# Gated cross-attention in four layers: the block of value matmuls moved ahead of the pair's last row maximum in TensorE's order

## The reference

```
x = x + tanh(g_xattn[l]) * attention_l(layernorm(x), ctx_1024, ctx_1024)
x = x + tanh(g_ffn[l])   * ffn_l(layernorm(x))
```

```
scores = jnp.einsum('blhe,bshe->bhls', q, k)
A = jax.nn.softmax(scale * scores, axis=-1)
ctx = jnp.einsum('bhls,bshd->blhd', A, v).reshape(Bsz, Lq, H * E)
out = ctx @ Wo + bo
```

## Time and profile before

| | |
|---|---|
| time, three runs | 1059.38, 1055.20, 1058.17 us; median 1058.17 us |
| span of the profiled execution, first to last instruction | 1052.7 us (its device time is not given apart from this; the three runs lie 2.5 to 6.7 us above the span) |
| instructions in the trace | 17430 |
| PE busy | 971.8 us (92%), 6530 matmuls |
| PE weight loads | 574.6 us (55%) |
| DVE busy | 774.0 us (74%) |
| ACT busy | 488.9 us (46%) |
| POOL busy | 290.5 us (28%) |
| mean granted TensorE clock | 0.969 of 2.4 GHz |
| costliest groups | reductions L2343: 640 of 681 ns mean, 397.1 us; exponents L1208: 320 of 1022 ns, 312.3 us; maxima L1567: 640, of 477 and 494 ns mean; values L1601: 2560 in the trace, 381 ns mean |

### The profile page before, as it was taken

How to read it: one execution, slowest core, us unless ns; L and a number is a source line. 1 busy time by engine, 2 the same in 40 slices (tenths; PEclk the granted TensorE clock), 3 DMA queues, 4 the chain that set the end, 5 groups by cost and what they waited for, 6 DMA issues and landing times.

```text
span 1052.7 us, 17430 instructions
## 1 busy us (share of the span) xinstructions
PE 971.8 (92%) x6530; PEld 574.6 (55%) x6530; DVE 774.0 (74%) x1445; ACT 488.9 (46%) x708; POOL 290.5 (28%) x439
## 2 busy tenths in 40 slices
PE   8897987999999977999689999999999999899998
PEld 4333353444444454999254444445788788644446
DVE  4989888999999631454489899995664645699956
ACT  2672331477777721121027777776312212347763
POOL 3656710133343203002302433322500400013230
PEclk9998989999999977999899999999999999999999
DMA  6889912103320323995341233201254242110001
GB/s 205 271 266 311 361 35 69 43 25 115 124 86 23 98 85 115 327 374 186 90 150 47 63 84 83 62 9 42 87 192 141 84 140 100 28 45 13 8 2 40
DMA packets 79181, 121.81 MB, mean 116 GB/s; under 512 B 9733, under 2 KB 52904, under 8 KB 79090
## 3 DMA queue, kind: packets, MB, share of 16 engines
q1 hardware_dynamic: 59278, 79.29, 24.3%
q10 hardware_dynamic: 19044, 39.22, 10.7%
q0 software_dynamic: 768, 2.10, 0.6%
HBM read 92.10 MB, written 27.81 MB: 114 GB/s over the span
## 4 chain that ended last, share of the span: by engine, by line
PE 67%; DVE 20%; DMA 5%; issue 3%; ACT 2%; POOL 2%; SPq 0%; DVEq 0%; ACTq 0%; POOLq 0%
PE bank L1601 15%; PE bank L1567 15%; PE bank L1822 12%; DVE arena L2343 10%; PE st_bank L1752 4%; PE bank L1764 4%; DMA kparts<-arena 3%; PE st_bank L1586 3%; PE st_bank L1822 2%; PE bank L1361 2%; PE st_bank L1515 1%; PE bank L1655 1%; PE bank L1620 1%; DVE bnst L1925 1%; PE st_bank L1891 1%
## 5 line engine op out<-in xcount | busy, mean ns | idle before, releaser
L2343 DVE TENSOR_REDUCE arena<-bank 128x1 f32<-128x512 f32 x640 | 397.1, 681 | 33.7 <-PE bank L1567 32.8
L1208 ACT ACTIVATE arena<-st_bank 128x1024 f32<-128x1024 f32 x320 | 312.3, 1022 | 137.1 <-PE st_bank L1586 136.0
L1567 PE MATMUL bank<-g_a 64*128 64x512 f32 x480 | 181.5, 477 | 11.7 <-DVE arena L2343 3.3
L1601 PE MATMUL bank<-arena,vaug 128*9 128x256 f32 (+2 forms) x2560 | 168.5, 381 | 1.3 <-ACT arena L1208 1.3
L1567 PEld LDWEIGHTS bank<-g_a 64*128 64x128 f32 x480 | 73.2, 183 | 124.9 <-DVE arena L2343 100.3
L1822 PE MATMUL bank<-g_a,g_w 128*128 128x512 f32 x512 | 117.3, 390 | 1.1 <-POOL g_a L959 1.1
L1586 PE MATMUL st_bank<-g_a 64*128 64x512 f32 x480 | 115.3, 417 | 0.0
L1822 PEld LDWEIGHTS bank<-g_a,g_w 128*128 128x128 f32 x512 | 95.9, 188 | 21.9 <-POOL g_a L959 2.0
L926 POOL COPY arena<-arena 8x32 f32<-8x32 f32 x160 | 34.8, 217 | 259.4 <-issue 137.2
L1601 PEld LDWEIGHTS bank<-arena,vaug 128*9 128x9 f32 (+2 forms) x2560 | 55.8, 92 | 75.2 <-issue 39.7
L1567 PE MATMUL bank<-g_x,g_a 64*128 64x512 f32 x160 | 63.4, 494 | 9.6 <-DVE arena L2343 3.5
(11 more groups left out here) (329 smaller groups left out, 1442.3 us busy)
## 6 DMA issues: line engine op xcount, KB each, us to landing
arena<-in_glu_w SPq DMA_DIRECT2D x39, 512.0 KB, 3.2
arena<-kv_table SPq DMA_DIRECT2D x11, 1024.0 KB, 7.6
ctxT<-in_glu_w ACTq DMA_DIRECT2D x22, 512.0 KB, 5.9
arena<-in_w SPq DMA_DIRECT2D x20, 512.0 KB, 5.9
kparts<-arena ACTq DMA_DIRECT2D x12, 512.0 KB, 5.4
arena<-in_w ACTq DMA_DIRECT2D x12, 512.0 KB, 3.4
xnT<-kv_table SPq DMA_DIRECT2D x5, 1024.0 KB, 8.0
g_a<-kparts SPq DMA_DIRECT2D x24, 192.0 KB
```

The lines of the kernel that those rows point to most:

```text
L1208: act.activation(prob[sl % PROBS], st_bank[sl % 2][:], ACT.Exp, scale=scale).then_inc(exp_ready, 1)
L1567: pe.matmul(bank[TURN_BANKS[place % 3]], Qc[gi % KQ_BUFS][rows, qt * P:(qt + 1) * P], Kc[gi % KQ_BUFS][rows, half * CH:(half + 1) * CH], s ...
L1601: ins = pe.matmul(bank[7][at:at + dh + 1, 0:D], vaug[l][:, b * KT + 2 * m + i, h0 + hh, :], tiles[:, a], start=(m == 0 and i == 0), stop=( ...
L2343: dve.tensor_reduce(mxh[gi % 2][:, col, hf:hf + 1], bank[TURN_BANKS[place % 3]], AX.X, ALU.max).then_inc(max_red, 1)
```

## The change

In `schedule`, the call that adds the pair's last row maximum moves from in front of the values step to behind it. Nothing is added or removed, and the other engines' lists keep their order, since VectorE has no values step and ScalarE neither maxima nor values.

```diff
@@ -182,9 +182,9 @@
             steps.append(("score", g, kt))
-            maxima(LEAD + HG * sl)
             if sl % 2 and sl >= VALUES_LAG:
                 steps.append(("values", (sl - VALUES_LAG) // KT, (sl - VALUES_LAG) % KT // 2))
+            maxima(LEAD + HG * sl)
             if kt == COPY_SLOT and g:
                 steps.append(("copy", g - 1))
```

## The result

| | before | changed |
|---|---|---|
| median of six runs | 1057.04 us | 1083.68 us |
| lowest to highest | 1053.88 to 1059.38 | 1079.92 to 1088.68 |
| span of the profiled execution | 1052.7 us | 1078.2 us |
| mean granted clock | 0.969 | 0.974 |

The changed kernel is slower: ratio 1.0265, 95% interval 1.0238 to 1.0293. In medians it is 26.6 us, and the interval reaches from 25.2 to 31.0 us. The forecast was 1084, 25.9 us more.

A forecast was written before the change was run, and what follows sets the result against it. TensorE and VectorE waiting for each other bound the kernel at 2.68 us a pair; 119 lengths of 2.92 and 14 of 3.51 make 396.6 us against 370.7, adding 25.9 to 1058.2: 1084 us, range 1069 to 1091.

The forecast's parts named there:

- The closed chain: In the attentions, TensorE and VectorE wait for each other in turn; one loop sets a regular pair's 2.68 us.
- The wait removed: Before the values: the last maximum's 0.49 us and the 0.73 of first reduction and semaphore leave the path.
- The wait that takes its place: At the next pair's third maximum: waiting for the last reduction closes a new loop of 2.92 us, 0.24 more.
- Group's end: Pairs where VectorE finishes a group: its extra 0.38 us is hidden, so they go from 2.82 to 2.92.
- Context: Pairs with a context: four transposes add 0.59 us to the loop, 3.51 against 3.41; a gap up to 0.1 possible.
- Edges: Each layer's ends: first values 0.3 us earlier, tail 0.2 to 0.5 later; taken as zero, 1 us either side.
- The step from span to time: From profiled span to median time: the 5.5 us distance seen before the change is kept.
- Scores' weights loaded while M2 waits: Behind the pair's third maximum: early weight loads make pairs 2.81 us, total 1070; chance 0.08.
- Scores passing M2: Around the third maximum: scores pass it altogether, leaving the loop at 2.68 us, total 1058; chance 0.05.
- Nothing closes: In the pairs: no new loop forms and VectorE sets 2.48 us, 20 us less, total 1038; chance 0.06.
- The clock falls: In the attentions: TensorE idles more; half clock in a third of the pairs adds 53 us, about 1137; chance 0.05.
- 80% for TensorE: TensorE's busy share of a changed pair: 2.35 of 2.92 us, used to weigh whether the clock would drop.

The follow-up runs named there:

- e5: Kernel before the change, with each VectorE reduction over 256 of its bank's 512 columns; 1000.17 us, ratio 0.9483.
- e6: Changed kernel, with each VectorE reduction over 256 of its bank's 512 columns; 1035.11 us, ratio 0.9802 to the kernel before.
- e2: Kernel before the change, with the odd slot's scores put ahead of the pair's third maximum; 1052.42 us, ratio 0.9987.
- e1: Changed kernel, with the odd slot's scores put ahead of the third maximum, values still ahead of the last; 1059.31 us, ratio 1.0043 to the kernel before.
- e3: Changed kernel, with the third maximum ahead of the even slot's scores too; 1119.24 us, ratio 1.0601 to the kernel before.
- e9: Changed kernel, with the two waits on a new group's keys and queries moved ahead of the earlier group's last maximum; 1084.14 us in one run.
- e4: Kernel before the change, with the eight value matmuls cut into two halves, one each side of the next pair's first two maxima; 1044.64 us, ratio 0.9900.
- e7: Kernel before the change, with four of the eight value matmuls ahead of the pair's last maximum, four behind; 1057.63 us, ratio 1.0010.

## Why the prediction was right

**What bounds the kernel.** The closed chain, right: e5 and e6 show that one reduction of four is on it, e2 that the order of M2 and the scores doesn't matter while they are off it, e1 and e3 that scores cost as soon as they are on it.

**The wait removed.** Right. In the changed kernel the values follow the scores, and M3 follows the values by the 0.98 that they take.

**The wait that takes its place.** Right in place and in size: every term of the 2.92 is in the chain of the changed kernel, 0.69, 0.04, 0.50 and 0.23, 0.98, 0.48.

**Group's end.** The prediction had such a pair at 2.92, hidden. VectorE's L2348 and L2355 are hidden indeed: e9, which leaves them alone, has no long pair but those with contexts and a single one of 3.07. But the pair that holds a new group's first maximum took 2.98. The term left out was the two fulfilled waits in front of M2, 31 such lengths of 0.06, 1.9 us.

**Context.** 3.51 was forecast, with up to 0.1 on top. The lengths read 3.56 to 3.59, so 14 of them are 0.9 us more. The terms are not those of the prediction, though: in the chain of waits of two such pairs (222.85 to 226.42 is one) stand M0 and M1 one after the other (0.42, a gap of 0.03, 0.49), two scores 0.23, a gap of 0.12, the transposes 0.63, M2 0.43, two scores 0.23 and the values 0.98, and no reduction. A group has ended just before, and VectorE runs through such a pair without a gap. That 3.51 came out near is in part luck. The new groups' 1.9 us, the contexts' 0.9 and the last hundredths of 2.92 make the 3.4 us between 396.6 and 400.0. That is more than the 2.7 us which the prediction gave its sum as reading error.

**Edges and the rest.** Taken as zero. From a layer's first maximum to its first values it is 24.62 us before and 24.32 now in layer 1, 23.94 and 23.66 in layer 2: the 0.3 earlier that was named. From the last counted values to the next, the length rose from 1.87 to 2.11 us in layer 1, inside the 0.2 to 0.5 named. The profiled execution had 3.8 us less outside, so the span came out at 1078.2 with 1078.6 forecast. Two misses cancelled there, 3.4 us too few in the pairs and 3.8 us of scatter, and that is luck. Against the medians of six runs, 26.6, the forecast is 0.7 short; their interval, 25.2 to 31.0 us, holds the forecast's 25.9 and the 29.3 of the counted lengths alike.

**The step from span to time.** The prediction put 5.5 us between the two. The changed kernel's profiled execution had its own time, 1079.92, 1.7 us above its span. The median lies 5.5 above it because that execution was the shortest of the six. The number was right, what it stood for was not: it is the scatter of the executions.

**The rivals.** *Scores' weights loaded while M2 waits*: no, 287.74 and 287.75 in the weight loads. *Scores passing M2*: no. In all 139 pairs of the changed kernel that have an M2, none of the odd slot's scores was recorded as starting ahead of it. The prediction's "program order that holds everywhere I looked" was a reading too strong all the same: behind the 283.00 of the earlier trace rows stand two records, the slot's second score at 282.995 and its first at 283.225, and the second is recorded as the earlier one in 152 of the 320 slots before. *Nothing closes*: no. *The clock falls*: no, 1.00 in all three stretches although VectorE idles 0.44 us of each pair and TensorE waits longer. The prediction's 80% for TensorE was added up from pieces and set beside the profile's busy time of two stretches, which is another measure: by the profile the changed kernel's first stretch is busy for 149.89 of 165.45 us, 91%, and the same stretch before for 149.58 of 153.17, 98%. e3, with pairs of 3.16 us, also stands at 1.00 in its layer 1, though its mean over the execution is 0.963.

## What to carry to other kernels

When two engines both wait for each other, write the loop down as a chain of instructions and semaphores from one iteration to the next, with the buffer's turn as one of its edges, and sum it; a move is worth what it puts on or takes off that sum, here to 0.01 us in a regular pair. Filling a visible wait with useful work did not help, because the instruction that had waited now came later, and the next turn of its buffer closed a longer loop: ask which instruction reuses the buffer of the one you delay, and what is queued behind it. What shortens such a loop is a smaller block on it, so cutting a long block in two where its neighbours are on the chain, and leaving it whole elsewhere, paid 2.1%.

## What the runs showed of the hardware

- Two waits on semaphores that are fulfilled long ago are not free: 0.06 us for the two on the critical chain of TensorE (e9, 2.98 to 2.92).
- A stalled maximum holds back the weight loads of what stands behind it even if half of the array is free: 287.74 and 287.75 in the changed kernel. At all 125 places of its trace where a maximum's weight load waited over 0.2 us for a reduction and scores stood next, their first load came 3 to 7 ns behind it. The Trainium skill (TensorE: Matmul & The Clock Gate, "Part 3: Packing small matmuls — row/col tiling") speaks of loads pulled ahead of matmuls in flight, not of matmuls that wait, so the trace bounds the rule and doesn't contradict it.
- Cutting a block of values in two costs about 0.12 us: one block is 0.98 us, two half blocks are 0.55 each (e4). For the whole pair the place of the cut counts: TensorE's own work is 2.42 us with the block whole (e5), 2.49 with M0 and M1 between the halves (e4), and 2.62 to 2.68 with M3 alone between them (e7). That the change between half of the array's rows and all of them is what costs was not tested by itself.
- Matmuls on different halves of the rows can be recorded as starting against program order: 282.995 us for a slot's second score, 283.225 for its first (kernel before).
